# First layer of a four-layer kernel: the tiles of maxima of a batch move from slots 0-15 of the step ahead to slots 4-15 of that step and 0-3 of its own

## What is computed

```python
q = xt @ Wq.T
qh = q.reshape(B, T, NH, dk).transpose(0, 2, 1, 3)
scores = scale * jnp.einsum('bhqd,bhkd->bhqk', qh, qh)
logits = (scores * cmask + (1.0 - cmask) * NEG) * rmask
attn = jax.nn.softmax(logits, axis=-1)
ctx = jnp.einsum('bhqk,bhkd->bhqd', attn, qh)
out = ctx @ Wo.T
```

## Time and profile before

| | us |
|---|---|
| median of 3 runs | 2805.89 |
| lowest, highest | 2802.98, 2807.58 |
| profiled execution | 2816.45 |
| its span | 2814.6 |
| TensorE busy in the span | 2633.3 |
| VectorE busy | 2097.5 |
| ScalarE busy | 1348.0 |
| GpSimd busy | 914.2 |

### The profile page before, as it was taken

The page is one execution under the profiler, slowest core; times in us unless marked ns, Lnnn a source line. Parts: engine busy times, 40 slices in busy tenths (PEclk is TensorE's granted clock), DMA queues, the critical chain, the costliest instruction groups (busy, mean ns, idle before and its releaser), DMA issues. The chain is left out here.

```text
span 2814.6 us, 108219 instructions
## 1 busy us (share of the span) xinstructions
PE 2633.3 (94%) x46966; PEld 1503.7 (53%) x46966; DVE 2097.5 (75%) x4263; ACT 1348.0 (48%) x2344; POOL 914.2 (32%) x830
## 2 busy tenths in 40 slices
PE   8999999999989999999999999997999999999986
PEld 4333333333379898989999898983222222222221
DVE  5766666666788887888888887755777777777785
ACT  2555555555322222222322222211888787887876
POOL 1444444444022222222222222111244344344333
PEclk9999999999799999999999999998999999999999
DMA  2310111101100000000000000004344444544532
GB/s 66 94 55 28 54 37 46 55 28 43 27 14 0 0 0 0 0 0 0 0 0 0 0 0 0 0 5 108 74 107 116 107 106 112 114 104 112 115 91 52
DMA packets 120897, 132.05 MB, mean 47 GB/s; under 512 B 31800, under 2 KB 84944, under 8 KB 120674
## 3 DMA queue, kind: packets, MB, share of 16 engines
q1 hardware_dynamic: 114942, 123.12, 17.1%
q10 hardware_dynamic: 5760, 6.56, 0.8%
HBM read 85.29 MB, written 44.30 MB: 46 GB/s over the span
## 5 line engine op out<-in xcount | busy, mean ns | idle before, releaser
L912 PE MATMUL exp_ps<-region,gru_hT 128*16 128x128 f32 x16384 | 498.5, 274 | 39.3 <-DVE gru_hT L1039 7.8
L1582 DVE TENSOR_REDUCE x<-exp_ps 128x2 f32<-128x1024 f32 x352 | 426.0, 1221 | 104.8 <-PE exp_ps L1693 104.3
L912 PEld LDWEIGHTS exp_ps<-region,gru_hT 128*16 128x16 f32 x16384 | 428.3, 103 | 107.8 <-DVE gru_hT L1039 107.8
L845 POOL TENSOR_TENSOR xT<-xT,gru_hT 128x64 f32<-128x64 f32 x256 | 181.0, 707 | 824.6 <-DVE gru_hT L1039 815.6
L1508 ACT ACTIVATE region<-exp_ps,x 128x1024 f32<-128x1024 f32 x336 | 370.2, 1110 | 72.8 <-PE exp_ps L1664 72.8
L407 POOL TENSOR_TENSOR l_probs<-l_probs 128x1024 f32<-128x1024 f32 x120 | 281.1, 2349 | 297.7 <-ACT l_probs L483 220.1
L958 ACT ACTIVATE gru_r<-exp_ps 128x128 f32<-128x128 f32 x256 | 70.9, 277 | 588.1 <-PE exp_ps L912 588.1
L593 DVE TENSOR_REDUCE l_maxes<-exp_ps 128x2 f32<-128x1024 f32 x176 | 214.9, 1221 | 132.8 <-PE exp_ps L668 132.7
L997 DVE SCALAR_TENSOR_TENSOR xT<-x,condT,xT 128x512 f32<-128x512 f32 x420 | 311.0, 781 | 0.0
L897 PE MATMUL exp_ps<-region,gru_x_st 128*32 128x128 f32 x8192 | 272.1, 274 | 11.4 <-POOL gru_x_st L863 11.4
L1677 PE MATMUL bank<-region,x 128*17 128x512 f32 x2048 | 271.5, 602 | 6.7 <-ACT region L1508 3.6
(11 more groups left out here) (182 smaller groups left out, 4240.7 us busy)
## 6 DMA issues: line engine op xcount, KB each, us to landing
region<-key_query_scratch SPq DMA_DIRECT2D x128, 192.0 KB
key_query_scratch<-x SPq DMA_DIRECT2D x48, 256.0 KB, 2.5
key_query_scratch<-region SPq DMA_DIRECT2D x48, 256.0 KB, 2.5
region<-in_x SPq DMA_DIRECT2D x16, 512.0 KB, 4.8
l_xres<-in_x SPq DMA_DIRECT2D x16, 512.0 KB, 4.0
x_scratch<-x SPq DMA_DIRECT2D x16, 512.0 KB, 2.8
l_rden<-rden_scratch SPq DMA_DIRECT2D x120, 64.0 KB, 2.1
l_rden<-rden_scratch SPq DMA_DIRECT2D x240, 32.0 KB, 1.8
```

Source lines behind the costliest of these rows:

```text
L845: pool.tensor_tensor(dst, dst, hT[:, q, :, HALF:QW], ALU.add).then_inc(added, 1)
L912: last = pe.matmul(out[QW * j:QW * j + rows, cols], hT[:, p, k, state], group_of(wh[:, k, gate, :], j), start=False, stop=True, skip_group ...
L1582: dve.tensor_reduce(maxes[:, half, qt, head % HH:head % HH + 2], pairs[ring.place[2 * slot + 1]][:, :, :], AX_X, ALU.max).then_inc(taken[" ...
```

## The change

Tiles of maxima are no longer bound to the slot with their number. `FIRST = 4` puts tile 0 of batch s+1 at slot 4 of step s, tile 11 at slot 15, and tiles 12 to 15 at slots 0 to 3 of step s+1, the batch's own. `tile_at(slot)` gives the tile and whether it is the step's own batch (0) or the next (1). Each half's split follows its eighth tile: slot 11 for the first half (7 before), slot 3 for the second (15 before). The tasks that hang on them move: mta from slot 10 to 13, mtb from 1 to 5, and out of their way v1 from 5 to 6, v0 from 13 to 14. On GpSimd the masks of the second half, which wait for mtb, move behind the first two of the step's eight sums. In step -1 there are 12 tiles of maxima instead of 16, in step 15 there are 4 instead of none.

```diff
-    AT = {"mtb": 1, "q1": 3, "v1": 5, "mta": 10, "q0": 11, "v0": 13, "out": 15, "reciprocal": 5, "sums": 10}
+    AT = {"mtb": 5, "q1": 3, "v1": 6, "mta": 13, "q0": 11, "v0": 14, "out": 15, "reciprocal": 5, "sums": 10}
+
+    FIRST = 4
...
+        def tile_at(slot):
+
+            return (slot - FIRST) % SLOTS, 0 if slot < FIRST else 1
+
...
-            order += [(slot, "st", slot, 0, 16), (slot, "max", slot, 1, 16)]
+            order += [(slot, "st", slot, 0, 16), (slot, "max", *tile_at(slot), 16)]
...
                 if active(s, 1):
                     set_masks(0, "mta", s + 1)
-                    set_masks(1, "mtb", s + 1)
-                if active(s, 0) and not (isinstance(s, int) and s == LAST):
-                    for n in range(SEGS // 2):
+                for n in range(SEGS // 2):
+                    if n == 1 and active(s, 1):
+
+                        set_masks(1, "mtb", s + 1)
+                    if active(s, 0) and s != LAST:
                         for hp in range(2):
                             add_tiles(s, n, hp)
...
-                    if active(s, 1):
-                        half, qt, hp = max_tile(slot)
-                        wait(dve, ready["max"], 16 * (s + 1) + slot + 1)
-                        if slot % 8 == 0:
+                    tile, ahead = tile_at(slot)
+                    if active(s, ahead):
+                        half, qt, hp = max_tile(tile)
+                        wait(dve, ready["max"], 16 * (s + ahead) + tile + 1)
+                        if tile % 8 == 0:
...
-                        if slot % 8 == 7:
-                            split(half, "mtb" if half else "mta", s + 1)
+                        if tile % 8 == 7:
+                            split(half, "mtb" if half else "mta", s + ahead)
...
-                if active(s, 1):
-                    if slot % 8 == 0:
-                        wait(pe, kq_done[half], s + 2)
+                if active(s, ahead):
+                    if tile % 8 == 0:
+                        wait(pe, kq_done[half], s + ahead + 1)
                     tasks.free(pe, s, at["max"])
+                    of = (par + ahead) % 2
...
-                        last = pe.matmul(tasks.bank(at["max"])[:, i, :], kq[rows, 1 - par, half, qt * P:qt * P + P],
-                                         kq[rows, 1 - par, half, :], start=True, stop=True)
+                        last = pe.matmul(tasks.bank(at["max"])[:, i, :], kq[rows, of, half, qt * P:qt * P + P],
+                                         kq[rows, of, half, :], start=True, stop=True)
```

More of the change, by code:

```diff
@@ L301, in l0_part, with max_tile @@
         block = ctx.enter_context(nc.Block())
-        def max_tile(slot):
-            return slot // 8, slot % 8 // 2, 1 - slot % 2
+        def max_tile(tile):
+            return tile // 8, tile % 8 // 2, 1 - tile % 2
         @block.sync
@@ L586, in step @@
                 for slot in range(SLOTS):
-                    if active(s, 1):
-                        half, qt, hp = max_tile(slot)
-                        wait(dve, ready["max"], 16 * (s + 1) + slot + 1)
-                        if slot % 8 == 0:
-                            wait(dve, split_done, 2 * s + half + 1)
-                        dve.tensor_reduce(maxes[:, half, qt, 2 * hp:2 * hp + 2], tasks.bank_of("max", slot)[:, :, :], AX_X, ALU.max)\
+                    tile, ahead = tile_at(slot)
[3 more added lines that the diff above has]
+                        if tile % 8 == 0:
+                            wait(dve, split_done, 2 * (s + ahead - 1) + half + 1)
+                        dve.tensor_reduce(maxes[:, half, qt, 2 * hp:2 * hp + 2], tasks.bank_of("max", tile)[:, :, :], AX_X, ALU.max)\
                            .then_inc(taken["max"], 1)
-                        if slot % 8 == 7:
-                            split(half, "mtb" if half else "mta", s + 1)
+                        if tile % 8 == 7:
+                            split(half, "mtb" if half else "mta", s + ahead)
                     for kind, idx, off in (("q1", 1, 1), ("q0", 0, 2)):
@@ L650, in products @@
                 grp, kt = seg // 4, seg % 4
-                half, qt, mp = max_tile(slot)
-                at = {kind: next(n for n, t in enumerate(tasks.tasks) if t[1] == kind and t[2] == slot) for kind in ("st", "max")}
+                tile, ahead = tile_at(slot)
+                half, qt, mp = max_tile(tile)
+                at = {kind: next(n for n, t in enumerate(tasks.tasks) if t[0] == slot and t[1] == kind) for kind in ("st", "max")}
                 if active(s, 0):
```

## The result

| | before | changed |
|---|---|---|
| median, us | 2805.65 (4 runs) | 2831.97 (4 runs) |
| lowest, highest | 2802.98, 2807.58 | 2826.81, 2837.15 |
| profiled execution | 2816.45 | 2837.15 |
| its span | 2814.6 | 2835.3 |

A forecast was written before the change was run, and what follows sets the result against it. TensorE, busy 94% of the span, was taken as the bound. Terms -4.4 - 0.5 + 33.0 + 0.5 - 2.0 = +26.6 us against the median of 2805.89 gave 2832.5 us, 0.95% slower; range 2816 to 2845.

The forecast's parts named there:

- What bounds the kernel; the split: First layer, slot 3: split ends about +5.97, after GpSimd's second sum, delaying slot 4's reduction; TensorE loses 1.0 us.
- Steady steps: First layer, each step: 1.0 (slot 3) + 1.0 and 0.3 (slot 11) - 0.1 = 2.2 us longer, bounds 1.5 and 2.6.
- The wait at slot 8: TensorE's 1.12 us wait for a bank of the exponentials was to stay, 0.1 to 0.2 shorter.
- Ahead of step 0: Step -1, with 12 tiles left: step 0 was to start at 47.4 instead of 51.76, -4.4 us.
- Steps 0 to 14: The 15 steps that each lose 2.2 us: +33.0 us.
- the border: Steps 0 and 1: a 0.79 us wait at step 1's start goes, mtb's 0.3 shows in step 0; together -0.5.
- rival 3: Steady steps: more stalls than counted, as idle time lowers the clock or small waits grow; 2850 and more, chance 0.06.
- Step 15 and the clock: Last step: +0.5 us for small waits, and -2 for a later fall of TensorE's clock, bounds -8 and +4.
- (1): Rival, slot 3: VectorE gets in before GpSimd's sum and the split holds up nothing; 2802.5, chance 0.09.
- The tie at slot 3: The cast is ready at +2.69 and GpSimd's second sum can start between +2.65 and +2.70.
- (2): Rival: a wait at slot 5 gives slots 6 to 8 back what they lose, shrinking slot 8's stall; 2800, chance 0.03.
- (4): Rival, steady steps: the stalls are there but about half as large; +12, 2817, chance 0.12.

## Why the prediction was right

**What bounds the kernel; the split.** The whole forecast hung on one reading of the earlier trace rows: a small cast beside a sum is held to the sum's end, the chain of four begins there, and the reduction of the next slot has no slack. The cast ends 0.06 us after the sum, the split 0.97 after it (334.48 against 333.51), the transposes start at +7.81, the reduction of slot 3 starts 1.48 into the slot. Each is within 0.05 us of its number, and the experiments with late splits, short sums, an added split and late sums (the masks back) confirm the cause from four sides.

**Steady steps.** 2.20 us of 2.2, and by half 1.01 and 1.28 of 1.0 and 1.3. The wait at slot 8 stayed (1.08 after 1.12, where 0.1 to 0.2 less was counted).

**Ahead of step 0.** -5.05 where -4.4 was predicted. The first tile starts at 21.58 and not at 22.1, since the four keep-busy pairs of the empty slots run on from one another (16 products from 17.98 to 19.77, 1.79 us where 2.1 was counted); the rest is 25.13 against 25.3. Small, and not the main point. Half the clock in this step, in three of the nine profiled executions with 12 tiles and in none of the three with 16, was not foreseen; so few don't show that the change makes it more likely.

**Steps 0 to 14.** +34.2 where 32.5 was predicted, with the border. In step 0 the clock of the changed kernel's profiled execution fell:

```profile
52.00:59.00 7.00, 6.91 (x28) 1.99 (x29) 2.30 (x3) 1.72 (x3) 2.34 (x1) 0.55 0.26 75
```

7 us at 0.55 cost up to 3 us (an estimate from the two levels), enough for the 1.7: step 0 is 4.3 us longer than before and not 2.5, the others sum to what was worked out. It is rival 3's mechanism, once and not in each step: from there to step 15 the clock stays at 1.00 with 3 us of waits in a step.

**Step 15 and the clock.** -3.4 where 0.5 - 2.0 = -1.5 was predicted, within its bounds; the clock is 0.84 granted from 735 to 800 us, 0.77 in the same stage before (705 to 773). The split and mtb did fit: the split ends at 746.76, 12.3 us into the step (12.4 was worked out), and the transpose at 749.98 doesn't wait. But this term can't be called confirmed. From its start to the end of the layer's last output, step 15 took 67.9 us in the kernel before, 68.0 and 57.2 in its two variants with an added split and an added cast, whose step 15 is the same code; in the changed kernel it took 64.5, in its two variants with the masks back, again with the same step 15, 58.0 and 64.5. One code spreads by 11 us, more than the -2 and about as much as the bounds given to it.

**The rivals.** (1) The tie at slot 3 goes to GpSimd's sum: the median cast of 2.37 us says so. The Trainium skill, SBUF — State Buffer, section Who interferes with whom, says that the port is held for one whole instruction and goes by order of issue; by that rule the sum came out the same whoever won. The trace agrees that a whole instruction is waited for (a cast of 2.37 us that ends 0.06 after the sum). No run shows the whole chain getting ahead of a sum that is ready with it; the kernel with the late splits (43.63 a step) comes nearest to what it would have meant. (2) The wait at slot 8 gives nothing back: 1.08 us are left of it, as the exponential came later too. (4) The stalls are not half as large: 0.94 each.

**Luck.** The profiled execution's difference is 20.7 us, that of the medians 26.3, the sum's 26.6. The layer itself accounts for 25.7; that the medians agree with the sum to 0.3 us is better than the sum's terms, which miss by 0.7, 1.7 and 1.9 with different signs. The 25.7 has luck in it as well: it compares one execution of each kernel, step 15 alone can move either by 11 us, and that of before was a slow one, 10.8 us above its median. What is earned is the 33 us of the steady steps; the rest of the sum is smaller than what the clock does from one execution to the next.

## What to carry to other kernels

Before a chain of small VectorE instructions is moved, look at what GpSimd runs at the new place, and ask which of the instructions behind it in the queue hands a bank back to TensorE: the chain did not cost its length alone here (1.11 us, which would have fitted into a wait of 1.32), it cost its last four instructions after the end of GpSimd's work. If what stands behind was blocked by the same sum anyway, the first instruction is nearly free, and the others are not. Two slots later the same chain cost nothing here, and the move paid a little (ratio 0.9986, interval up to 0.9999). Where a stage loses TensorE work, look at its clock in more than one execution before the work saved is counted as gained.

## What was not expected of the hardware

- One wait of 5 us in a step of 52 lowered TensorE's clock behind it: the granted clock was 0.93 over that step, and the 15 steps took 31.8 us less, the median 26 us, when dummy products filled the wait. Two waits of 0.94 and one of 1.08 in 46 us did not: 1.00.
- In step -1, a program with waits of 0.25 to 0.69 us and TensorE otherwise busy kept its clock in one execution and had it at half for 17 us in another. Step 0 started 8.2 us later with it. What decides it is open.
- The cast of 128 x 16 took 0.20 us alone, 0.74 behind a sum over 128 x 256 and 2.37 behind one over 128 x 1024, and was recorded as running from 0.04 us after the short sum's start to 0.06 after its end: the time that it was held up counts as busy. Recorded VectorE time that falls (25 us here) can therefore be nothing but waiting that has moved elsewhere.
